# First-layer experts and shared MLP on Trainium2: the 96-wide remainders of gate and up in shared stationaries, the last 64 rows of down in two output halves

## The reference

```
logits = x_tokens @ router_w + router_b          # 16 experts, top 2
C = ceil(1.25 * 2048 * 2 / 16)                   # 320 slots for each of 16 experts
_mlp(h, wg, wu, wd) = silu(h @ wg) * (h @ wu) @ wd      # 256 -> 352 -> 256
expert_outputs = vmap(_mlp)(expert_inputs, w_gate, w_up, w_down)
out = x + _mlp(x, sw_gate, sw_up, sw_down) + gathered expert outputs * gate
```

## Time and profile before

| | |
|---|---|
| median of 3 runs | 1119.5 us (1118.37 to 1121.49) |
| the profiled execution: span from first to last instruction | 1118.0 us |
| mean granted TensorE clock over the span | 0.992 |
| PE busy / DVE / ACT / POOL | 1073.2 / 488.1 / 525.8 / 320.7 us |
| layer 0's experts on PE | about 233 to 423 us of the span |

### The profile page before, as it was taken

How to read it: one execution, slowest core, us unless ns; L and a number is a source line. 1 busy time by engine, 2 the same in 40 slices (tenths; PEclk the granted TensorE clock), 3 DMA queues, 4 the chain that set the end, 5 groups by cost and what they waited for, 6 DMA issues and landing times.

```text
span 1118.0 us, 23799 instructions
## 1 busy us (share of the span) xinstructions
PE 1073.2 (96%) x7550; PEld 906.5 (81%) x7550; DVE 488.1 (44%) x2591; ACT 525.8 (47%) x1904; POOL 320.7 (29%) x317
## 2 busy tenths in 40 slices
PE   8999997999999999899998799999999999999996
PEld 7788876876666668677776699999999999999995
DVE  5779997622222323568988422222222222222221
ACT  2999999421112112999998033333323333332331
POOL 3222533413433442003226512222212222221222
PEclk9999999999999999999999899999999999999998
DMA  9932010156566644049101199999999998999980
GB/s 329 379 127 76 21 40 36 44 153 176 115 173 153 137 81 94 1 137 361 35 27 44 56 349 322 313 307 318 311 312 320 316 314 304 310 315 318 319 283 10
DMA packets 152006, 219.06 MB, mean 196 GB/s; under 512 B 15422, under 2 KB 124437, under 8 KB 151408
## 3 DMA queue, kind: packets, MB, share of 16 engines
q1 hardware_dynamic: 132976, 203.41, 53.2%
q0 software_dynamic: 18944, 14.62, 7.4%
HBM read 184.74 MB, written 43.09 MB: 204 GB/s over the span
## 4 chain that ended last, share of the span: by engine, by line
PE 79%; ACT 9%; DVE 3%; issue 3%; SPq 2%; DMA 2%; POOL 1%; POOLq 0%; DVEq 0%; ACTq 0%
PE bank L1075 21%; PE bank L1088 19%; PE bank L944 9%; PE bank L954 6%; ACT probs L1151 5%; PE bank L831 3%; PE bank L799 3%; PE bank L912 3%; PE bank L921 2%; PE bank L822 2%; PE bank L845 2%; PE bank L775 2%; PE bank L808 1%; PE bank L872 1%; PE bank L930 1%
## 5 line engine op out<-in xcount | busy, mean ns | idle before, releaser
L1318 ACT ACTIVATE dhidT<-bank,b1T 128x128 f32<-128x128 f32 x512 | 145.9, 368 | 308.9 <-PE bank L1075 308.9
L1075 PE MATMUL bank<-probsT,arena 128*128 128x128 f32 x2048 | 240.9, 277 | 0.1
L1075 PEld LDWEIGHTS bank<-probsT,arena 128*128 128x128 f32 x2048 | 235.5, 193 | 0.4 <-DVE probsT L1738 0.3
L1088 PE MATMUL bank<-arena,dhidT 128*128 128x256 f32 x1024 | 231.5, 380 | 0.0
L1088 PEld LDWEIGHTS bank<-arena,dhidT 128*128 128x128 f32 x1024 | 190.1, 191 | 22.9
L747 POOL DMA_INDIRECT out<-probsT,slot_token x64 | 98.6, 1540 | 375.5 <-DMA out<-probsT,slot_token 299.1
L1151 ACT ACTIVATE probs<-probs,neg_max 128x128 f32<-128x128 f32 x512 | 197.7, 393 | 1.6 <-DVE neg_max L1424 1.4
L1756 DVE TENSOR_TENSOR probsT<-bank,b_wide 128x256 f32<-128x256 f32 x64 | 27.2, 425 | 346.3 <-PE bank L1088 346.3
L1424 DVE CUSTOM_DVE_ANT_0 probs<-bank,mask 128x128 f32<-128x128 f32 x512 | 112.7, 284 | 11.6 <-PE bank L822 11.1
L718 POOL DMA_INDIRECT stream<-arena,slot_token x48 | 72.6, 1513 | 128.9 <-DVE arena L1618 94.7
L944 PE MATMUL bank<-rowsT,arena 128*128 128x320 f32 (+1 forms) x384 | 108.9, 436 | 0.2 <-DVE arena L1609 0.2
(11 more groups left out here) (162 smaller groups left out, 1368.7 us busy)
## 6 DMA issues: line engine op xcount, KB each, us to landing
arena<-L_ffn_w SPq DMA_DIRECT2D x128, 1024.0 KB, 7.3
rows<-zeros SPq DMA_DIRECT2D x13, 1024.0 KB, 12.1
drows<-rows SPq DMA_DIRECT2D x64, 132.0 KB, 7.5
arena<-L_ffn_w_gate SPq DMA_DIRECT2D x16, 352.0 KB, 4.4
arena<-L_ffn_w_up SPq DMA_DIRECT2D x16, 352.0 KB, 5.5
early<-rows SPq DMA_DIRECT2D x16, 264.0 KB, 3.5
early<-x SPq DMA_DIRECT2D x8, 512.0 KB, 6.8
arena<-L_ffn_w_down SPq DMA_DIRECT2D x16, 256.0 KB, 2.8
```

Of the source, the lines that this page charges most:

```text
L1075: mm = pe.matmul(bank[2 + 2 * (u % 2) + half][:, jj * P:(jj + 1) * P], w1_sb[u][:, c, j * P:(j + 1) * P], drowsT[:, u % 2, c, :], start=c ...
L1088: last_ = pe.matmul(bank[6 + u % 2][:, 0:D], dhidT[:, u % 2, j, :], w2_sb[u][:, j, :], start=j == 0, stop=j == J1 - 1)
L1318: last_ = act.activation(dhidT[:, u % 2, j, :], bank[2 + 2 * (u % 2) + half][:, jj * P:(jj + 1) * P], ACT.Gelu, bias=b1T[:, j, bass.ds(e, 1)])
```

## The change

Gate and up weights come as one array, L0_ffn_w_gate_up, made on the host in column order gate 0:128, up 0:128, gate 128:256, up 128:256, gate 256:320, up 256:320, gate 320:352, up 320:352 (704 columns); the same for the shared MLP. So one DMA loads them where two did. For j = 0 and 1 nothing else changes. For j = 2 one stationary of 128 columns holds 64 of gate and 64 of up, and a last one of 64 columns holds 32 of gate and 32 of up; with the latter the 320 slots (256 tokens) go in two halves, written to partitions 0:64 and 64:128 of the columns behind. ACT applies silu to all of it at once, DVE multiplies in three pieces. `down(e, 2)`, which has 64 slots, writes output columns 0:128 to partitions 0:64 and 128:256 to partitions 64:128, and `result_b(e, 2)` takes two pieces.

```diff
@@ load_gate_up
-                sp.dma_start(gate_w[u], a["L0_ffn_w_gate"][bass.ds(e, 1)].rearrange("a (c p) f -> p (a c) f", c=DC)).then_inc(s, 16)
-                sp.dma_start(up_w[u], a["L0_ffn_w_up"][bass.ds(e, 1)].rearrange("a (c p) f -> p (a c) f", c=DC)).then_inc(s, 16)
+                sp.dma_start(gate_up_w[u], a["L0_ffn_w_gate_up"][bass.ds(e, 1)].rearrange("a (c p) f -> p (a c) f", c=DC)).then_inc(s, 16)
@@ gate_up
-                for w, dst in ((gate_w[e % 2], score_bank[2 * (n % 2)]), (up_w[e % 2], score_bank[2 * (n % 2) + 1])):
+                w, dst = gate_up_w[e % 2], score_bank[2 * (n % 2):2 * (n % 2) + 2]
+                if j < 2:
+                    for half in range(2):
+                        f = (2 * j + half) * P
+                        for c in range(DC):
+                            last = pe.matmul(dst[half][:, 0:C0], w[:, c, f:f + P], rowsT[:, e % 2, c, :], start=c == 0, stop=c == DC - 1)
+                else:
                     for c in range(DC):
-                        last = pe.matmul(dst[0:m, 0:C0], w[:, c, f:f + m], rowsT[:, e % 2, c, :], start=c == 0, stop=c == DC - 1)
+                        pe.matmul(dst[0][:, 0:C0], w[:, c, TAIL:LAST], rowsT[:, e % 2, c, :], start=c == 0, stop=c == DC - 1)
+                    for c in range(DC):
+                        for part_ in range(2):
+                            last = pe.matmul(dst[0][64 * part_:64 * (part_ + 1), C0:C0 + CH], w[:, c, LAST:2 * F0],
+                                             rowsT[:, e % 2, c, CH * part_:CH * (part_ + 1)],
+                                             start=c == 0, stop=c == DC - 1, skip_group_check=True)
@@ down
-                    last = pe.matmul(bk[0:m, 0:D], hidT[e % 2][0:fm, j, r:r + m], down_w[e % 2][0:fm, j, :], start=j == 0, stop=j == NFT - 1)
+                    if s < 2:
+                        last = pe.matmul(bk[0:m, 0:D], hidT[e % 2][0:fm, j, r:r + m], down_w[e % 2][0:fm, j, :], start=j == 0, stop=j == NFT - 1)
+                    else:
+                        for c in range(DC):
+                            last = pe.matmul(bk[64 * c:64 * (c + 1), 0:P], hidT[e % 2][0:fm, j, r:r + m], down_w[e % 2][0:fm, j, c * P:(c + 1) * P],
+                                             start=j == 0, stop=j == NFT - 1, skip_group_check=True)
@@ silu_b
-                act.activation(silu[n % 2][0:m, :], score_bank[2 * (n % 2)][0:m, 0:C0], ACT.Silu).then_inc(e_silu, 1)
+                size = C0 if j < 2 else C0 + CH
+                act.activation(silu[n % 2][:, 0:size], score_bank[2 * (n % 2)][:, 0:size], ACT.Silu).then_inc(e_silu, 1)
@@ hidden_b
-                dve.tensor_tensor(hidT[e % 2][0:m, j, :], silu[n % 2][0:m, :], score_bank[2 * (n % 2) + 1][0:m, 0:C0], ALU.mult).then_inc(e_hid, 1)
+                if j < 2:
+                    last = dve.tensor_tensor(hid[:, j, :], act_[:, 0:C0], second[:, 0:C0], ALU.mult)
+                else:
+                    dve.tensor_tensor(hid[0:64, j, :], act_[0:64, 0:C0], first[64:P, 0:C0], ALU.mult)
+                    for part_ in range(2):
+                        at_ = 64 * part_
+                        last = dve.tensor_tensor(hid[64:64 + FQ, j, CH * part_:CH * (part_ + 1)], act_[at_:at_ + FQ, C0:C0 + CH],
+                                                 first[at_ + FQ:at_ + 2 * FQ, C0:C0 + CH], ALU.mult)
@@ result_b
-                dve.tensor_scalar(yrows[e % 4][0:m, s, :], job_bank[b][0:m, 0:D], slot_gate[0:m, e, s:s + 1], None, ALU.mult).then_inc(job_free[b], 1)
+                if s < 2:
+                    last = dve.tensor_scalar(yrows[e % 4][0:m, s, :], job_bank[b][0:m, 0:D], slot_gate[0:m, e, s:s + 1], None, ALU.mult)
+                else:
+                    for c in range(DC):
+                        last = dve.tensor_scalar(yrows[e % 4][0:m, s, c * P:(c + 1) * P], job_bank[b][64 * c:64 * (c + 1), 0:P],
+                                                 slot_gate[0:m, e, s:s + 1], None, ALU.mult)
```

More of the change, by code:

```diff
@@ L145, in build @@
     B = 2 * PAIRS
-    NE0, _, F0 = a["L0_ffn_w_gate"].shape
+    NE0, F0, _ = a["L0_ffn_w_down"].shape
     NE1, _, F1 = a["L1_ffn_w1"].shape
@@ L255, in build @@
         all_inT = part(DC * N).rearrange("p (c n) -> p c n", c=DC)
-        gate_w = [part(DC * F0).rearrange("p (c f) -> p c f", c=DC) for _ in range(2)]
-        up_w = [part(DC * F0).rearrange("p (c f) -> p c f", c=DC) for _ in range(2)]
+        gate_up_w = [part(DC * 2 * F0).rearrange("p (c f) -> p c f", c=DC) for _ in range(2)]
         down_w = [part(NFT * D).rearrange("p (j d) -> p j d", j=NFT) for _ in range(2)]
         hidT = [part(NFT * C0).rearrange("p (j n) -> p j n", j=NFT) for _ in range(2)]
-        silu = [part(C0) for _ in range(2)]
         yrows = [part(NCT * D).rearrange("p (s d) -> p s d", s=NCT) for _ in range(4)]
         shT = [part(NFT * 2 * P).rearrange("p (j n) -> p j n", j=NFT) for _ in range(2)]
-        sh_act = [part(2 * P) for _ in range(NFT)]
+        sh_act = [part(2 * P), part(2 * P), part(3 * P)]
         w1_sb = [arena[:, s * SLOT1:s * SLOT1 + DC * F1].rearrange("p (c f) -> p c f", c=DC) for s in range(RING1)]
@@ L295, in build @@
             rowsT = ctx_b.enter_context(nc.sbuf_tensor("rowsT", [P, 2, DC, C0], F32))
+            silu = [ctx_b.enter_context(nc.sbuf_tensor(f"silu{u}", [P, C0 + CH], F32)) for u in range(2)]
         tok = early[:, 4 * D:6 * D].rearrange("p (t d) -> p t d", t=2)
@@ L1192, in shared_silu @@
             def shared_silu(p, j):
-                f, m = FT[j]
                 wait_read(act, SHARED, (p - 1, GATE_UP + j))
                 bk, _ = from_job(SHARED, p, GATE_UP + j)
-                act.activation(sh_act[j][0:m, :], bk[0:m, 0:D], ACT.Silu).then_inc(sh_silu, 1)
+                n = D if j < 2 else D + P
+                act.activation(sh_act[j], bk[:, 0:n], ACT.Silu).then_inc(sh_silu, 1)
             def keep_rows(e, c):
@@ L1605, in hidden_b @@
                 n = NFT * e + j
-                f, m = FT[j]
                 dve.wait_ge(e_silu, n + 1)
                 wait_written(dve, EXPERTS, (e - 2, DOWN + 2))
-                dve.tensor_tensor(hidT[e % 2][0:m, j, :], silu[n % 2][0:m, :], score_bank[2 * (n % 2) + 1][0:m, 0:C0], ALU.mult).then_inc(e_hid, 1)
+                hid, act_, (first, second) = hidT[e % 2], silu[n % 2], score_bank[2 * (n % 2):2 * (n % 2) + 2]
+                if j < 2:
+                    last = dve.tensor_tensor(hid[:, j, :], act_[:, 0:C0], second[:, 0:C0], ALU.mult)
[5 more added lines that the diff above has]
+                                                 first[at_ + FQ:at_ + 2 * FQ, C0:C0 + CH], ALU.mult)
+                last.then_inc(e_hid, 1)
             def result_b(e, s):
@@ L1617, in result_b @@
                 b, _ = EXPERTS.jobs[e, DOWN + s]
-                dve.tensor_scalar(yrows[e % 4][0:m, s, :], job_bank[b][0:m, 0:D], slot_gate[0:m, e, s:s + 1], None, ALU.mult).then_inc(job_free[b], 1)
+                if s < 2:
+                    last = dve.tensor_scalar(yrows[e % 4][0:m, s, :], job_bank[b][0:m, 0:D], slot_gate[0:m, e, s:s + 1], None, ALU.mult)
+                else:
+                    for c in range(DC):
+                        last = dve.tensor_scalar(yrows[e % 4][0:m, s, c * P:(c + 1) * P], job_bank[b][64 * c:64 * (c + 1), 0:P],
+                                                 slot_gate[0:m, e, s:s + 1], None, ALU.mult)
+                last.then_inc(job_free[b], 1)
             def shared_hidden(p, j):
-                f, m = FT[j]
                 dve.wait_ge(sh_silu, NFT * p + j + 1)
@@ L1625, in shared_hidden @@
                 b, _ = SHARED.jobs[p, GATE_UP + j]
-                dve.tensor_tensor(shT[p % 2][0:m, j, :], sh_act[j][0:m, :], job_bank[b][0:m, D:2 * D], ALU.mult).then_inc(job_free[b], 1)
+                bk = job_bank[b]
+                if j < 2:
+                    last = dve.tensor_tensor(shT[p % 2][:, j, :], sh_act[j], bk[:, D:2 * D], ALU.mult)
+                else:
+                    dve.tensor_tensor(shT[p % 2][0:64, j, :], sh_act[j][0:64, 0:D], bk[64:P, 0:D], ALU.mult)
+                    for t in range(2):
+                        at_ = 64 * t
+                        last = dve.tensor_tensor(shT[p % 2][64:64 + FQ, j, t * P:(t + 1) * P], sh_act[j][at_:at_ + FQ, D:D + P],
+                                                 bk[at_ + FQ:at_ + 2 * FQ, D:D + P], ALU.mult)
+                last.then_inc(job_free[b], 1)
             def shared_add(p):
@@ L1798 @@
         arrays[name] = np.ascontiguousarray(w.reshape(w.shape[0] // P, P, w.shape[1]).transpose(1, 0, 2))
-    a = {name: nc.dram_tensor(name, arrays[name].shape, F32, kind="ExternalInput").ap() for name in NAMES}
+    for part in ("w", "sw"):
+        gate, up = arrays.pop(f"L0_ffn_{part}_gate"), arrays.pop(f"L0_ffn_{part}_up")
+        cuts = ((0, P), (P, 2 * P), (2 * P, 2 * P + P // 2), (2 * P + P // 2, gate.shape[-1]))
+        arrays[f"L0_ffn_{part}_gate_up"] = np.ascontiguousarray(
```

(2 more changed lines are left out.)

32 lines of the change are left out of this document (19 added, 13 removed).

## The result

The changed kernel takes 1113.6 us (median of 5 runs, 1111.66 to 1119.95) beside 1119.3 us for the kernel before on the same chip (5 runs, 1118.37 to 1121.49): ratio of the two 0.9952, 95% interval 0.993 to 0.9973. A second set of six runs, `changed_again`, gave 1114.98 us and 0.9949 (0.9933 to 0.9965). So the change is worth 5 to 6 us. Forecast was 11.3, with a range that ended at 1113.5: the direction was right, the size about half.

What follows compares the result with a forecast made beforehand. PE's column streaming was taken to bound the expert stage. Terms -3.3 - 10.4 - 0.3 + 1.7 + 0.5 + 0.5 = -11.3 us take the 1118.0 span to 1106.7, plus 1.5 for the median: 1108.2 us, range 1104.5 to 1113.5.

Steps and rivals of the forecast that it cites:

- the wait for weights: Expert stage: the single gate and up DMA may land late for a faster PE; +0.5 us, between 0 and 1.
- the shared pieces on ACT and DVE: Attention stretches: longer shared silu and multiplications lie mostly beside other work; at most 2.5 us, taken as +0.5.
- a factor of two for two halves: PE matmuls: two 64-column parts run at once, twice as fast, inferred from four 32-column parts at L845.
- 0.35 us a visit: PE: going to the narrow array shape costs 0.14 us and coming back 0.21.
- Rivals 1: PE: each narrow part must finish before the next starts, so the kernel turns slower, 1129.3 us; chance 0.05.
- Rival 2: PE: loads of a part do not hide behind its neighbour's matmuls, 53 ns exposed each; 1117.3 us; chance 0.05.
- rival 3: Expert stage: DVE becomes last to arrive everywhere, 0.8 us lost per expert; 1119.3 us, no change; chance 0.07.
- By the median 0.4 us of slack stays: Expert weights: 1.2 us of slack by median landing time, less 0.65 + 0.18 us that PE loses before use.
- +1.7: Expert stage: PE stands still for longer DVE hidden pieces, 0.8 us each at down(7, 0) and down(13, 0); +1.7 us.
- -3.3: Expert gate_up(e, 2), 16 times: 0.18 us saved each, plus 0.35 once where two narrow runs meet; -3.3 us.
- Behind the experts: Start of layer 1: 1.1 us of slack before PE loads normed hides the h reload, so the gain travels unchanged.
- Rival 4: After the experts: the h reload or layer 1 sets its own date, half the gain lost, about 1114; chance 0.03.

Runs made afterwards that it cites:

- changed_again: The changed kernel once more with no edit, timed beside the kernel before: 1114.98 us, ratio 0.9949.
- no_shared: The changed kernel with the shared MLP's functions and weight arrays as in the kernel before, experts as changed: 1110.85 us, ratio 0.9915.
- shared_kept: The full change, shared MLP included, with two swaps in DVE's list and SP's earlier row and gate/up weight loads: 1109.45 us, ratio 0.9904.
- experiment 5: Both repaired load and DVE orders tried in other kernels; here shared_kept with shared_hidden(5, 2) ahead of front_c(L1, 0) on DVE: 1110.86 us, ratio 0.9919.
- down_moved_loads: The kernel before with only the down and result_b change, plus two DVE swaps and SP's earlier loads: 1108.67 us, ratio 0.9897.
- two_dmas: The changed kernel with each expert's gate and up weights split into two DMAs, load order kept: 1112.66 us, ratio 0.993.

## Why the prediction was wrong

In short: the matmuls were forecast rightly, and two costs around them were put far too low, the wait for weights (+0.5, measured +3.0) and the shared pieces on ACT and DVE (+0.5, and in net with their matmuls +0.2, measured some +3 to +4). That the measured time ended only 0.1 us outside the range is no merit: its upper end was a sum of bounds of which these two did not hold.

**What held.** That the expert stage is PE's columns; a factor of two for two halves; 0.35 us a visit; `down` at -10.4 (measured -10.5); `gate_up(e, 2)` at 1.97 us. Rivals 1 and 2 are refuted by the chain, rival 3 by waits for DVE of 2.5 us in all, not over 5. Rival 2 was priced too low besides: a load of 64 columns takes 132 to 139 ns, not 53, since its length is not in proportion to its columns (110 ns for 32 of them). Rival 2 is also what the Trainium skill (TensorE: Matmul & The Clock Gate, Part 3) would have: a load hides only behind a matmul in another row group. Here both halves use the same rows, their loads last 132 to 139 ns, and twelve of them with twelve matmuls take 0.81 us in all. The measurement speaks against the rule for column halves.

**First step that failed: "By the median 0.4 us of slack stays".** I set the slack of the weights by a median landing time over 14 transfers. The waits are decided by the transfers that are late, and for these the trace before had the landings: expert 4's at 275.34 for a use at 275.68, expert 11's at 357.87 for 358.51. Slack was 0.34 and 0.64 us, against 0.83 us or more lost by PE's speed. For expert 4 the sum can be redone. SP's chain of loads is set off by the end of `down(1, 2)`: SP issues at 266.64 before,

```profile
266.64 0.37 SPq L513 DMA_DIRECT2D arena<-L_ffn_w_down  x1
```

and at 267.32 in the profile after, whose whole expert stage starts 2.3 us later. Between `down(1, 2)` and the use PE lost 0.84 us, as forecast. The weights were issued 0.28 us later behind it than before, and landed 0.56 us later behind their issue. Together 1.68, less the slack of 0.34, and with the 0.25 from landing to start: a wait of 1.6 us by the starts of PE's operations, 1.52 in the row. So the forecast had PE's part right, and missed the true slack and the slower loads. The term of 0.5 us measured 3.0 in `changed_again` (1.7 + 1.3) and 3.4 in the profile after.

**A step that was missing: what PE loses behind a wait.** The eight matmuls behind the two waits took 4.07 and 3.60 us for 2.39 in `changed_again`, in part at half the clock: 2.8 us more between starts. These falls come in some executions only: the profile after has three up to 428 us, one of them in layer 0's attention, `changed_again` none up to there, and its expert stage is 4.3 us shorter. The profiled execution being also the longest of its five, they are a likely cause of its length: its mean granted clock is 0.987, that of the other four 0.989 to 0.990. What spreads those four from 1111.66 to 1115.66 us is not shown.

**Second step that failed, the larger in size: "mostly beside other work: at most 4 x 0.6 = 2.5 us, I take +0.5"** for the shared pieces. They stood in the path, with a bank that PE was waiting for. The part costs 4.1 us by `no_shared` (3.8 by the ratios); `shared_kept` has 3.2 (2.0 by the ratios, with intervals that overlap). About 1.5 us are in its own path: 0.8 until the expert stage, 0.7 behind it. By the profiles the rest went with falls of the granted clock, of which the upper end of 2.5 us knew nothing, and whose cause stays open.

**Smaller.** DVE: 0.81 us for the hidden pieces, not 0.5, so 2.26 us at two `down` and some 0.2 at two more for the +1.7. Gate and up: -2.4 for -3.3. *Behind the experts*: the cover of 1.1 us held for h, but `shared_hidden(5, 2)` stands on DVE behind that reload, and PE waited 0.7 us for it; moving it (experiment 5) changed nothing, as the reload is next in line. `down_moved_loads`, without the shared part, waits 0.6 us there too, so it is PE's earlier arrival as much as the longer pieces. Rival 4 was thus right in kind for that fraction.

**The sum as `changed_again` has it**, by the starts of PE's operations: +0.8 us until the expert stage begins (shared pieces in layer 0), -7.8 in the stage (-2.4 - 10.5, and some 5.1 of waits that were not there), +0.8 from its end to layer 1's first turn, -0.2 to the second, +1.9 between the second and third turn (nearly all with the clock, see `shared_kept`). That is -4.5, and its last matmul ends 4.5 us earlier than before (1103.08, 1107.57).

## What to carry to other kernels

Where an engine that is never idle is made faster, look up for each transfer and each value its own arrival beside its own use: the median said nothing about the two that came late here. Make the order of the queues part of the change: two swaps on DVE and loads issued one expert ahead brought 4.6 us in the medians (3.2 by the ratios) on top of the 9 to 10 of the same matmuls. A part whose forecast gain is 0.3 us and that lengthens a chain on other engines is better left out (it cost 3 to 4). A new wait on PE may cost up to about twice its length: the one of 1.5 us had 1.6 us of slower matmuls behind it, the one of 1.9 us 1.2. And before two profiles are compared, look where each one's clock fell: between the profiles of `changed_again` and `two_dmas` two such places made 2.6 us, more than most terms of this forecast.

## What the runs showed of the hardware

Two output halves of 64 partitions run side by side at a full factor of two at 128 and at 160 columns, with loads hidden. On DVE, pieces are dear: a multiplication of 320 columns takes 476 to 490 ns, one of 160 still takes 316 to 327. The granted clock fell to its lower level behind PE's waits of 1.5 and 1.9 us, for 3 to 4 us each time, while the two waits of 1.06 us had no fall behind them, nor had the waits of 1.27 and 1.70 us for the same weights in `changed_again`. In `no_shared` a wait of 1.68 us had one. What decides between the two stays open.
